# A graph-attention kernel: break rows stored once and on other tiles, statistics tile by tile, type one-hots for two groups at a time

## The reference, cut to what matters

```python
xn = _layernorm(x, axis=-1)
# in _L0_gnn_ref(xn, ...):
rel = rel_w[edge_relations]
mod_k = K[src] + 0.2 * rel[:, None, :]
scores = jnp.einsum('ehd,ehd->eh', Q[dst], mod_k) / D ** 0.5
seg_max = jax.ops.segment_max(scores, dst, num_segments=N)
ex = jnp.exp(scores - seg_max[dst])
denom = jax.ops.segment_sum(ex, dst, num_segments=N)
w = ex / denom[dst]
agg = jax.ops.segment_sum(w[:, :, None] * V[src], dst, num_segments=N)
```

## Time and profile before

| | |
|---|---|
| median of 3 runs | 1360.5 us (1359.99 to 1361.61) |
| the profiled execution | 1360.95 us |
| its span, first to last instruction | 1359.1 us |
| busy share PE, DVE, ACT, POOL | 83%, 69%, 60%, 57% |
| mean granted TensorE clock | 0.923 of full speed |
| projection stage | 0 to about 199 us |
| edge stage | about 200 to 885 us |

### The profile page before, as it was taken

How to read it: one execution, slowest core, us unless ns; L and a number is a source line. 1 busy time by engine, 2 the same in 40 slices (tenths; PEclk the granted TensorE clock), 3 DMA queues, 4 the chain that set the end, 5 groups by cost and what they waited for, 6 DMA issues and landing times. The chain is left out here.

```text
span 1359.1 us, 26561 instructions
## 1 busy us (share of the span) xinstructions
PE 1123.6 (83%) x7285; PEld 867.0 (64%) x7286; DVE 939.8 (69%) x2100; ACT 816.7 (60%) x2868; POOL 776.2 (57%) x853
## 2 busy tenths in 40 slices
PE   5999926899999999999999998756775589999950
PEld 3777724566666666666666666545653379999940
DVE  7676327999999999999999999346563812122215
ACT  3444300588888888888888888512342066776630
POOL 4666347777777777777777774033220644554520
PEclk9999966799999999999999999989985789999985
DMA  7332358888788888878778775092101822221218
GB/s 224 114 104 98 109 111 254 237 236 230 234 227 235 227 236 233 232 231 231 231 232 233 229 234 155 0 328 81 39 20 61 257 59 70 66 69 66 69 37 281
DMA packets 132710, 225.06 MB, mean 166 GB/s; under 512 B 23555, under 2 KB 89098, under 8 KB 132594
## 3 DMA queue, kind: packets, MB, share of 16 engines
q0 software_dynamic: 43456, 138.49, 34.9%
q1 hardware_dynamic: 89138, 85.16, 20.7%
HBM read 191.18 MB, written 32.40 MB: 165 GB/s over the span
## 5 line engine op out<-in xcount | busy, mean ns | idle before, releaser
L572 POOL DMA_INDIRECT KV<-kv,ixs x464 | 494.4, 1065 | 142.6 <-issue 139.6
L587 ACT ACTIVATE KV<-KV,WS 128x65 f32<-128x65 f32 x1792 | 453.6, 337 | 22.5 <-ACT RR L613 17.0
L677 PE MATMUL ps_o<-KV,PM 128*128 128x260 f32 x928 | 256.2, 399 | 25.8 <-DVE PM L772 12.8
L677 PEld LDWEIGHTS ps_o<-KV,PM 128*128 128x128 f32 x928 | 158.7, 190 | 73.8 <-DVE PM L772 29.5
L658 PE MATMUL ps_qe<-Q,PT 128*128 x1392 | 199.6, 282 | 5.2 <-DVE KV L761 5.2
L658 PEld LDWEIGHTS ps_qe<-Q,PT 128*128 128x128 bf16 x1392 | 138.7, 100 | 55.2 <-issue 8.5
L683 PE MATMUL ps_o<-ACC,ident 128*128 x464 | 154.2, 414 | 0.0
L761 DVE TENSOR_TENSOR KV<-KV,ps_qe 128x512 f32<-128x512 f32 x232 | 148.4, 667 | 0.2
L754 DVE TENSOR_TENSOR KV<-KV,ps_u 128x1024 f32<-128x1024 f32 x116 | 139.6, 1204 | 6.9 <-DMA KV<-kv,ixs 6.9
L1491 DVE TENSOR_TENSOR YG<-ps_y,B 128x256 f32<-128x256 f32 x56 | 23.8, 425 | 170.1 <-PE ps_y L1465 170.1
L767 DVE TENSOR_REDUCE S<-KV 128x16 f32<-128x1024 f32 x116 | 139.4, 1202 | 2.0
(11 more groups left out here) (300 smaller groups left out, 1685.3 us busy)
## 6 DMA issues: line engine op xcount, KB each, us to landing
dlb<-dl_rows SPq DMA_DIRECT2D x116, 128.0 KB
W<-in_f_W_dram SPq DMA_DIRECT2D x16, 512.0 KB, 6.2
tyb<-ty_rows SPq DMA_DIRECT2D x116, 64.0 KB
KV<-kv,ixs POOLq DMA_INDIRECT x464, 4.3
kv<-kvb SPq DMA_DIRECT2D x25, 258.0 KB, 2.3
xs_rows<-xs SPq DMA_DIRECT2D x25, 256.0 KB, 2.4
YF<-ytab SPq DMA_DIRECT2D x8, 640.0 KB, 9.2
VB<-kv SPq DMA_DIRECT2D x5, 650.0 KB, 9.1
```

The lines of the kernel that those rows point to most:

```text
L572: pool.indirect_dma_start(kv[:, c % KR, n, :], None, d["kv"], bass.IndirectOffsetOnAxis(ap=T["ixs"][:, c % KR, n:n + 1], axis=0)).then_inc ...
L587: m = a.activation(part, part, ACT.Copy, scale=W[:, c % 2, s * H + h:s * H + h + 1])
L677: m = pe.matmul(T["ps_o"][:, p % 2, 0:A], PM[:, p // 2 % 2, p % 2 * 2 + k, :], kv[:, c % KR, 2 * x + k, C:KVW], start=(k == 0), stop=False)
```

## The change

Four things change.

1. **Break rows.** `brk` holds the rows once. They are stored by one DMA (116 partitions of 4 KB), after tile 17; one `links` store follows after each of tiles 18 to 21, and `dl0` after tile 22. In the edge stage the load of the break rows becomes 4 loads a chunk, one for each head, into every fourth partition, each beside one `links` load.
2. **Statistics.** Chunk 1 stays on tile 1. For the rest, each of the tiles 2 to 17 has one `bn_stats` and one `bn_aggr` (`tile_statistics`), behind the normalising and ahead of the evacuation. The square root moves behind ScalarE's exponent of tiles 7, 12 and 17, and `inverse` (two instructions, one fewer) to the front of tiles 8, 13 and 18.
3. **Type one-hots.** The two halves of the 128 partitions hold the types of two groups, so one operation of 128 x 512 (on every even group) takes the place of two of 64 x 512. The type table `rel3` lies in both halves; TensorE's `relations` reads its group's half. PT and OT have semaphores of their own: `relations` waits for OT, `queries` for PT.
4. The gathers' semaphores are 6 in place of 12.

```diff
             def step_breaks():
                 sp.wait_ge(s_brk, 1)
-                for h in range(H):
-                    sp.dma_start(d["brk"].rearrange("(p q h) w -> p q h w", q=Q, h=H)[:, :, h, :],
-                                 T["PEN"][0:R, :, :, :].rearrange("p q t e -> p q (t e)")).then_inc(s_st, 16)
-                for t in range(4):
-                    sp.dma_start(d["links"][t].rearrange("(p q) -> p q", q=Q), EL[0:R, t, :]).then_inc(s_st, 16)
+                sp.dma_start(d["brk"].rearrange("(p q) w -> p q w", q=Q), T["PEN"][0:R, :, :, :].rearrange("p q t e -> p q (t e)")).then_inc(s_st, 16)
+
+            def step_links(t):
+                sp.dma_start(d["links"][t].rearrange("(p q) -> p q", q=Q), EL[0:R, t, :]).then_inc(s_st, 16)
+
+            def step_first():
                 sp.dma_start(d["dl0"], T["dl0"][0:R, 0:1]).then_inc(s_st, 16)
...
-                if i == STEPS_AT + 13:
+                if i == STEPS_AT + 11:
                     step_breaks()
+                if STEPS_AT + 12 <= i < STEPS_AT + 16:
+                    step_links(i - STEPS_AT - 12)
+                if i == STEPS_AT + 16:
+                    step_first()
...
+                inverse(c)
+
+            def inverse(c):
+                t0, t1 = c * XT_, (c + 1) * XT_
                 v.wait_ge(s_a, c + 1)
                 q(v.reciprocal(rstd[:, t0:t1], rstd[:, t0:t1]))
-                q(v.tensor_tensor(nmr[:, t0:t1], T["mv"][:, t0:t1, 0], rstd[:, t0:t1], ALU.mult))
-                q(v.tensor_scalar(nmr[:, t0:t1], nmr[:, t0:t1], -1.0, None, ALU.mult))
+                q(v.scalar_tensor_tensor(out=nmr[:, t0:t1], in0=T["mv"][:, t0:t1, 0], scalar=-1.0, in1=rstd[:, t0:t1], op0=ALU.mult, op1=ALU.mult))
+
+            def tile_statistics(t):
+
+                c, k = divmod(t, XT_)
+                if t - 1 >= 2 * XT_:
+                    v.wait_ge(s_v, q.n)
+                    v.bn_aggr(T["mv"][:, t - 1, :], T["stats"][:, t - 1, :]).then_inc(s_v, 1)
+                    q.n += 1
+                if t < NT:
+                    v.wait_ge(s_x[c], 16)
+                    v.bn_stats(T["stats"][:, t, :], X[:, t, :]).then_inc(s_v, 1)
+                    q.n += 1
+                if k == 0 and c > 2:
+                    v.wait_ge(s_v, q.n)
+                    b = slice((c - 1) * XT_, c * XT_)
+                    v.tensor_scalar(rstd[:, b], T["mv"][:, b, 1], EPS, None, ALU.add).then_inc(s_sq, 1)
...
             step_list()
             constants()
             for i in range(NT):
-                if i % XT_ == 1 and i // XT_ + 1 < XQ:
-                    statistics(i // XT_ + 1)
+                if i == 1:
+                    statistics(1)
+                if i % XT_ == 3 and 2 <= i // XT_ + 1 < XQ:
+                    inverse(i // XT_ + 1)
                 if i + 2 < NT:
                     normalise(i + 2)
+                if i >= 2 and i + 8 <= NT:
+                    tile_statistics(i + 8)
                 evacuate(i, i % 2)
...
             for i in range(NT):
                 if i + 1 < NT:
                     copy_turned(i + 1, (i + 1) % 2)
-                if i % XT_ == 1 and i // XT_ + 1 < XQ:
+                if i == 1:
+                    deviation(1)
+                parts(i, i % 2)
+                if i % XT_ == 2 and 2 <= i // XT_ + 1 < XQ:
                     deviation(i // XT_ + 1)
-                parts(i, i % 2)
...
         def _(sp):
             def rows(G_):
                 h = G_ % 2
-                wait(sp, s_oh, 2 * (G_ - 1))
+                wait(sp, s_oh, G_ - 1)
                 s0 = G_ * G // 2
                 sp.dma_start(T["dlb"][:, h, :], d["dl_rows"][s0:s0 + G // 2, :].rearrange("s e -> (s e)").unsqueeze(0).broadcast_to([P, G * P])).then_inc(s_bc[h], 16)
-                sp.dma_start(T["tyb"][:, h, :], d["ty_rows"][s0:s0 + G // 2, :].rearrange("s e -> (s e)").unsqueeze(0).broadcast_to([NREL, G * P])).then_inc(s_bc[h], 16)
-
-            def breaks(c):
+                if h == 0:
+                    m = G_ // 2
+                    wait(sp, s_ot, m - 1)
+                    for j in range(2):
+                        s1 = s0 + j * G // 2
+                        sp.dma_start(T["tyb"][j * NREL:(j + 1) * NREL, m % 2, :],
+                                     d["ty_rows"][s1:s1 + G // 2, :].rearrange("s e -> (s e)").unsqueeze(0).broadcast_to([NREL, G * P])).then_inc(s_bt[m % 2], 16)
+
+            def breaks(c, g):
                 wait(sp, s_sm, (c - 1) * SMV)
-                sp.dma_start(T["BR"][:, c % 2, :, :], d["brk"][c * B:(c + 1) * B, :].rearrange("r (t e) -> r t e", t=4)).then_inc(s_bl[c % 2], 16)
-                for t in range(4):
-                    sp.dma_start(T["ET"][0:1, c % 2, t, :, 1:CB_ + 1],
-                                 d["links"][t:t + 1, c * CB_:(c + 1) * CB_].unsqueeze(1).broadcast_to([1, H, CB_])).then_inc(s_bl[c % 2], 16)
+                sp.dma_start(T["BR"][g::H, c % 2, :, :], d["brk"][c * CB_:(c + 1) * CB_, :].rearrange("r (t e) -> r t e", t=4)).then_inc(s_bl[c % 2], 16)
+                sp.dma_start(T["ET"][0:1, c % 2, g, :, 1:CB_ + 1],
+                             d["links"][g:g + 1, c * CB_:(c + 1) * CB_].unsqueeze(1).broadcast_to([1, H, CB_])).then_inc(s_bl[c % 2], 16)
...
                 for g in range(CG):
                     if c * CG + g + 2 < NG:
                         rows(c * CG + g + 2)
-                breaks(c)
+                    breaks(c, g)
...
             def relations(G_):
                 h = G_ % 2
-                pe.wait_ge(s_oh, 2 * G_ + 2)
+                half = slice(h * NREL, (h + 1) * NREL)
+                pe.wait_ge(s_ot, G_ // 2 + 1)
                 wait(pe, s_ku, G_ - 1)
                 for k in range(G):
                     for n in range(3):
-                        m = pe.matmul(T["ps_u"][:, h, k * D:(k + 1) * D], T["OT"][:, h, k * P:(k + 1) * P], T["rel3"][:, n, :],
+                        m = pe.matmul(T["ps_u"][:, h, k * D:(k + 1) * D], T["OT"][half, G_ // 2 % 2, k * P:(k + 1) * P], T["rel3"][half, n, :],
                                       start=(n == 0), stop=(n == 2))
...
             def queries(p, at):
                 h = p // 2 % 2
+                pe.wait_ge(s_oh, p // 2 + 1)
                 wait(pe, s_mu, p - 2)
...
             def onehots(G_):
                 h = G_ % 2
-                v.wait_ge(s_bc[h], 32 * (G_ // 2 + 1))
+                v.wait_ge(s_bc[h], 16 * (G_ // 2 + 1))
                 wait(v, s_qe, 2 * (G_ - 1))
                 v.tensor_scalar(T["PT"][:, h, :], T["dlb"][:, h, :], T["iota_p"][:, 0:1], None, ALU.is_equal).then_inc(s_oh, 1)
-                v.tensor_scalar(T["OT"][:, h, :], T["tyb"][:, h, :], T["iota_p"][0:NREL, 0:1], None, ALU.is_equal).then_inc(s_oh, 1)
+                if h == 0:
+                    m = G_ // 2
+                    v.wait_ge(s_bt[m % 2], 32 * (m // 2 + 1))
+                    v.tensor_scalar(T["OT"][:, m % 2, :], T["tyb"][:, m % 2, :], T["iota_t"][:, 0:1], None, ALU.is_equal).then_inc(s_ot, 1)
```

35 lines of the change are left out of this document (20 added, 15 removed).

## The result

The change is faster: 1330.0 us median (1326.8 to 1330.8, 4 runs) against 1360.2 (1359.5 to 1361.6, 4 runs) of the kernel before, a ratio of 0.977, 95% interval 0.975 to 0.979. The forecast was 1322.5, with a range of 1315 to 1336.5. The profiled execution took 1330.76 (span 1329.0), 30.2 less than the profiled one before.

The account below looks back on a forecast made before the run. VectorE was taken to bound the edge stage, with GpSimd's gathers close, and TensorE to pace the projection stage. 1360.95 - 19.8 (breaks) - 4.6 (statistics) - 13.7 (one-hots) = 1322.9, stated as 1322.5 us; range 1315 to 1336.5.

Parts of the forecast that it names:

- Breaks: Projection stage, tiles 22 to 23: storing break rows once removes the whole excess wait for tile 20's stores, 19.8 us gained.
- Rival 2: Projection stage: the five small stores each delay their tile, 7 us in all, giving 1329.5 us; chance 0.08.
- Rival 3: Tile 20's stores: not held by the bytes of brk, so 10 us of stall remain, giving 1332 us; chance 0.04.
- Statistics: Projection stage: spreading statistics over tiles removes 7.3 us and adds 2.7, net 4.6 us gained.
- The four excesses: Time over 5.83 us in front of tiles 6, 11, 16 and 17: 1.31, 2.45, 1.9 (assumed) and 1.69, together 7.3 us, which goes.
- The 0.7 and 0.6 for the table load: Tiles 9 and 14: ScalarE reloads the exponent's table after the square root, making them late by 0.7 and 0.6 us.
- The start: Kernel start: one more 16 KB load and two tiny VectorE instructions lie beside the weight loads, costing 0.
- One-hots: Edge stage: 58 OT operations replace 116, saving VectorE 13.7 us, or 0.52 a chunk.
- 54 x 0.26 - 0.3: Edge stage: 54 saved OT operations at 0.26 us each, less 0.3 for the larger shape: 13.7 us.
- Rival 1: Edge stage: gathers bind, the one before PM of g = 0 is caught, chunk stays 22.1, giving 1336 us; chance 0.2.
- Rival 4: Edge stage, slower: each chunk's four PMs catch a gather for 0.88 us, chunk 23.5, giving 1375 us; chance 0.03.
- the forecast case: Whole kernel: all three gains arrive as counted, 1322.5 us, within 1316 to 1328; chance 0.65.

Follow-up runs that it names:

- the swap: Changed kernel with VectorE's rescale moved behind the backward scan of g = 0 in the edge stage: 1452.3 us, 0.987 of the kernel before on the second chip.
- the swap with the separate semaphore: Changed kernel with rescale behind the backward scan and a semaphore of its own for the type-row loads: 1451.6 us, 0.988 of the kernel before, second chip.

## Why the prediction came out as it did

1. **Breaks**, -19.8 forecast, -20.2 measured. The size and the place were right. The reason, bytes that go at 96 GB/s, is half of it: the pile is the other half, since three copies more cost 13.6 us in one pile and 5.7 spread. Rival 2, that small stores hold the tiles, did not show in the changed kernel. In the old place one copy and the small stores together held a tile for 6.1 us (the rival had 7), and which of them did it stays open. Rival 3 has nothing left.
2. **Statistics**, -4.6 forecast, -5.4 measured. The four excesses went (tiles 6, 11, 16 and 17 come 5.87 or 6.0 behind the tile before). They were 7.6 us and not 7.3: tile 16, which was taken as 1.9, had 2.2 (8.00 - 5.83). What came instead is 0.5 in front of tile 4 (7.91 against 7.41) and 1.2 in front of tiles 8 and 13 each (7.31 and 7.28), 2.9 where I had 2.7, but the tile behind each of them comes 0.4 sooner, which I had not seen. The 0.7 and 0.6 for the table load at tiles 9 and 14 did not come. VectorE itself is late at tiles 8 and 13, so ScalarE loads the table beside it, and L396 waits for the exponent 0.78 and 0.97, where it waits 0.92 at other tiles. The `inverse` cost more than the 0.4 that I had, 0.83 and 0.67 up to the normalising; at tile 8 its second instruction took 0.58:

   ```profile
   74.36 0.18 DVE L263 RECIPROCAL rstd<-rstd 128x5 f32<-128x5 f32 x1
   74.57 0.58 DVE L264 SCALAR_TENSOR_TENSOR nmr<-mv,rstd 128x5 f32<-128x5 f32 x1
   75.19 0.78 DVE L286 TENSOR_SCALAR xnb<-X,rstd,nmr 128x256 f32<-128x256 f32 x1
   ```

3. **The start**, 0 forecast, +1.8 in the profile. I looked at the duration of what was added and not at which operation is then caught by the clearing of ACC.
4. **One-hots**, -13.7 forecast, about half measured. This is the step that failed, though the total stayed in the range. "54 x 0.26 - 0.3" counted every saved operation as time, because VectorE was busy for 22.03 of 22.1. That holds for g = 2. At g = 0 the cover was thin: rescale had followed ScalarE's copy by 0.20 with hardly a wait before (3.4 us in 2 waits over the whole run), so it was already at its earliest, and time won between `factors` and it could only turn into a wait. After the change it is 9.6 us in 28 waits. I had looked for the next limit at GpSimd, and had not followed ScalarE. That the wait, and not something behind it, costs the 0.24 is read from the traces; the experiment meant to show it, the swap, could not do so on the second chip, and it stays argued.
5. **Rival 1** (gathers bind): refuted on the first chip, 16 gathers fit in each typical chunk and the one at 0.12 got through. Rival 4's collisions did not come: 16.94 and 17.19 us of gathers in a chunk.
6. **The range.** 1330.0 lies in it, but above the 1316 to 1328 of the forecast case, and what raised it, ScalarE's chain and the start, is in none of the four rivals. That the range held is in part luck: it reached to 1336 for rival 1, which did not happen.

The Trainium skill ("SBUF — State Buffer", "SBUF: two separate sides") has the first starter hold the shared pair of ports for its whole instruction and block the other, a VectorE instruction with two SBUF inputs only against a GpSimd instruction that reads SBUF. The gather does read there, its indices `ixs`. I had taken half of this rule, that the gather goes through. By the other half PM, the second starter, would have been held until the gather's end at 513.18, 0.8 us later than it started. It was not: it started at 512.35 and took its usual 0.68. The same goes for the gather at 517.38 in the kernel before, which I had counted as agreeing. So the trace bears the rule out for neither pair; that the gather got through was forecast rightly, but this rule does not explain it. Nor does the rule fit VectorE's 0.17 us copy at 15.99 in the changed kernel's start: GpSimd's gather had begun at 15.88, by the rule the copy would have been held until 17.15 at least, and it was not.

No version that beats the changed kernel beyond doubt was found: the swap with the separate semaphore is at 1451.6 against 1455.2, and the intervals overlap.

## What to carry to other kernels

An engine that is busy for all of its time can still be at the earliest moment that another engine allows, at one place of its stream. Before counting a saved instruction as time, go through the waits behind it with their slack, those too that are too short to be listed as waits: here the first one without slack gave half of the saving back. Stores that hold a loop when they are issued in a row cost less when they are spread over its rounds, but look for the rest of their cost behind the loop's end too: three copies more cost 13.6 us in a row, and 5.7 spread, of which 3.5 came after the last tile. And a gain read from one chip should be given with what bounds the stage there: the one-hots went with a gain of some 7 us on one and, alone, cost 12.7 on another.

## What the runs showed of the hardware

The first chip and the second differ by 8% on the kernel before and by 9% on the changed one. In the changed kernel's profiles the difference lies wholly in the edge stage: its chunk is 21.8 us on one and 25.3 on the other, with the projection stage equal to a few tenths. The slower chips' late signals of TensorE, in bursts some 2 us behind their weight loads, are what differs in the records. What delays them was not found. In the changed kernel's profile on the second chip the chunks in which TensorE's clock falls to the lower level are 30.0 to 30.3 us long against 25.3, and the one looked at had its stall first and the fall 2.4 us into it.

In the run with one copy in the old place, a VectorE copy of 0.17 us took 6.59. It had started 0.24 behind the start of a gather of the edge list, and the clearing of ACC was queued behind that gather. In other profiles operations that started 0.14, 0.32 and 0.35 behind that gather were caught in the same way, and those at 0.03, 0.12 and 0.13 passed. Behind the gather ahead of it, which has no clearing behind it, operations at 0.11, 0.31 and 0.52 passed, so the time since a gather's start alone does not decide it. And the issue of a small store took SyncE up to 2.3 us with a copy of the break rows and other small stores right ahead of it, and 0.4 to 0.6 in the changed kernel.
